# A graph and attention layer: the pass over node rows is taken into the blocks of the edge sort

## What is computed

```python
xn = layernorm(x)
h = xn @ W_layer.T + b_layer            # 6250 x 256, gathered once an edge
a1 = h @ w_a1.T + b_a1;  a2 = h @ w_a2.T + b_a2
v = leaky_relu(a1[src] + a2[dst])       # softmax over the edges of a src
gnn = segment_sum(att[:, None] * h[dst], src)
q, k = (elu(xn @ w + b) + 1 for the q and the k weights)
kv, k_sum = k.T @ v of each head, sum over nodes of k
x = x + gnn + (q @ kv / (q @ k_sum)) @ wo + bo
x = x + ffn(layernorm(x))
```

## Time and profile before

| | us |
|---|---|
| median of 3 runs | 2029.47 |
| the profiled execution | 2033.18 |
| its span, first to last instruction | 2031.4 |
| busy in it: PE / DVE / POOL / ACT | 1497.9 / 1424.6 / 1080.7 / 628.8 |
| mean granted PE clock, share of full | 0.855 |

### The profile page before, as it was taken

How to read it: one execution, slowest core, us unless ns; L and a number is a source line. 1 busy time by engine, 2 the same in 40 slices (tenths; PEclk the granted TensorE clock), 3 DMA queues, 4 the chain that set the end, 5 groups by cost and what they waited for, 6 DMA issues and landing times. The chain is left out here.

```text
span 2031.4 us, 28833 instructions
## 1 busy us (share of the span) xinstructions
PE 1497.9 (74%) x8525; PEld 1175.0 (58%) x8525; DVE 1424.6 (70%) x4324; ACT 628.8 (31%) x1738; POOL 1080.7 (53%) x1147
## 2 busy tenths in 40 slices
PE   5555555348878758887888877887877878887699
PEld 3333333247767636666666666666666666665477
DVE  7888888865555538777777777877777778776244
ACT  0000000024344315444444444444444445442000
POOL 0245555501111057777777777777777777771000
PEclk8666666579999959888889899989998999989689
DMA  9500000001111134444444444444444444451622
GB/s 118 93 3 4 3 4 3 3 21 47 48 47 47 44 97 118 116 126 118 118 121 123 117 117 121 119 117 117 128 117 117 116 123 119 120 146 37 237 83 73
DMA packets 118495, 180.08 MB, mean 89 GB/s; under 512 B 41704, under 2 KB 90395, under 8 KB 118364
## 3 DMA queue, kind: packets, MB, share of 16 engines
q0 software_dynamic: 44384, 113.26, 21.7%
q1 hardware_dynamic: 62891, 45.40, 10.4%
q10 hardware_dynamic: 11088, 19.87, 2.6%
HBM read 143.16 MB, written 35.29 MB: 88 GB/s over the span
## 5 line engine op out<-in xcount | busy, mean ns | idle before, releaser
L978 POOL DMA_INDIRECT big<-node_table,rest x850 | 853.2, 1004 | 243.9 <-issue 231.2
L1049 PE MATMUL psum<-big 128*125 128x257 f32 x1700 | 460.4, 431 | 107.1 <-DVE big L1511 107.1
L1049 PEld LDWEIGHTS psum<-big 128*125 128x125 f32 x1700 | 360.0, 217 | 179.2 <-DVE big L1511 114.0
L1183 ACT ACTIVATE rest<-big,rest 128x125 f32<-128x125 bf16 x850 | 268.3, 490 | 184.4 <-DVE rest L1459 184.4
L321 POOL DMA_INDIRECT edge_groups<-rest x112 | 170.7, 1524 | 188.8 <-DVE rest L691 159.0
L1511 DVE TENSOR_SCALAR big<-big,rest 128x125 f32<-128x125 bf16 x850 | 173.6, 294 | 0.0
L342 POOL TENSOR_TENSOR X<-X,big 125x256 f32<-125x256 f32 x50 | 31.8, 638 | 260.5 <-DVE rest L778 260.5
L400 PE MATMUL psum<-rest 128*128 128x128 f16 x784 | 84.7, 304 | 111.7 <-DVE rest L676 111.7
L400 PEld LDWEIGHTS psum<-rest 128*128 128x128 f16 x784 | 78.5, 143 | 123.6 <-issue 82.0
L1077 PE MATMUL psum<-rest,big 125*128 125x126 f32 x416 | 72.0, 326 | 91.9 <-DVE big L1430 91.7
L1466 DVE TENSOR_REDUCE rest<-rest 128x125 f32<-128x2125 f32 x50 | 118.3, 2367 | 30.4 <-ACT rest L1183 30.4
(11 more groups left out here) (377 smaller groups left out, 2793.3 us busy)
## 6 DMA issues: line engine op xcount, KB each, us to landing
big<-node_table,rest POOLq DMA_INDIRECT x850
slice_weights<-rest ACTq DMA_DIRECT2D x52, 252.0 KB, 3.0
big<-slice_weights ACTq DMA_DIRECT2D x25, 252.0 KB, 7.0
big<-slice_weights SPq DMA_DIRECT2D x25, 252.0 KB, 6.7
node_table<-rest SPq DMA_DIRECT2D x50, 126.0 KB
query_features<-rest SPq DMA_DIRECT2D x50, 125.0 KB, 2.0
rest<-query_features SPq DMA_DIRECT2D x50, 125.0 KB, 2.5
out_dram<-rest SPq DMA_DIRECT2D x50, 125.0 KB
```

The source lines that it names most:

```text
L978: pool.indirect_dma_start(Gt[:, u, q * TW:(q + 1) * TW], None, table, bass.IndirectOffsetOnAxis(ap=item[:, u, 2 * q:2 * q + 1], axis=0)).t ...
L1049: mm = pe.matmul(bank[bAgg][0:R, 0:D + 1], P[:, u, q, :], Gt[:, u, q * TW:q * TW + D + 1], start=q == 0, stop=q == Q - 1)
L1183: act.activation(V[:, :, q], O[:, u, q, 0:R], ACT.Copy, scale=score[:, u, q:q + 1]).then_inc(s_v, 1)
```

## The change

- **The pass over node rows** is cut into units of one tile, spread over sort blocks 2 to 13: five tiles in blocks 2 and 8, four in each other one (`UNITS`). PE runs the units between the sort's own steps: the first after `ranks(4n+3)`, the middle ones after `ranks(4n+5)`, the last between the two halves of `put`. ACT normalises, copies the transpose, makes both parts of k's feature and copies h, a2 and a1 out of PSUM; POOL adds the two parts and keeps their sum (`k_features`) between its scatters. DVE has no part in a unit. Biases come from a bf16 matmul with three rows (`ones3` by `row3`) ahead of each product, and `va` is part of `WT`, now 259 columns wide.
- `ranks(g)` waits on `chosen` instead of `selected`.
- Flags of items come from 50 columns and one matmul (`items`), in sort block 0; the statistics lie behind the first two sort blocks, unrolled; the bias rows and normalisers are made in block 1.
- **Query features** are no longer stored: the turned xn is (`xn_store`), with the same DMA size, and in the gather loop PE makes q of tile i+2 (`queries`), DVE its lower part (`query_below`), ACT the exponent (`query_exp`) and DVE the feature (`query_feature`) of tile i+1. `bo` is added in `mix` by a matmul, so POOL's L342 is gone.

```diff
+                    def k_features(t):
...
+                        pool.wait_ge(ke_done, t + 1)
...
+                        pool.tensor_tensor(ks[:, u, :], re[:, u, 0, :], re[:, u, 1, :], ALU.add).then_inc(ks_done, 1)
+                        pool.wait_ge(ks_done, t + 1)
...
+                        pool.tensor_tensor(ks_sum, ks_sum, ks[:, u, :], ALU.add).then_inc(acc_done, 1)
...
+                    for m in range(1, NB + 1):
+                        units = UNITS[m] if m < NB else []
+                        c = 0
+                        for i, t in enumerate(units):
+                            k_features(t)
+                            for _ in range(2 if i < 3 else 0):
+                                scatter(m - 1, c)
+                                c += 1
+                        for c in range(c, GC):
+                            scatter(m - 1, c)
...
-                    pool.wait_ge(weights_in, 16 * 15)
-                    for t in range(T):
-                        pool.wait_ge(xn_done, t + 1)
-                        pool.tensor_tensor(X[:, t, :], X[:, t, :], bo, ALU.add).then_inc(bo_added, 1)
...
-                            pe.wait_ge(selected, g - 1)
+                            pe.wait_ge(chosen, g - 1)
...
+                    def turn(t):
...
+                            pe.wait_ge(kr_done, 2 * t)
...
+                    def key_products(t):
...
+                        pe.wait_ge(ks_done, t + 1)
+                        for c in range(DC):
+                            mm = pe.matmul(bank[6][:, c * D:(c + 1) * D], ks[:, t % 2, c * 128:(c + 1) * 128], xn[:, t % 4, :],
+                                           start=t == 0 and c == 0, stop=t == T - 1, skip_group_check=True)
+                    def unit(t):
...
+                        u = t % 2
+                        pe.wait_ge(xnT_done, t + 1)
+                        pe.matmul(bank[0][0:R, D:2 * D], ones3, row3[:, BK_AT:BK_AT + D], start=True, stop=False)
+                        for c in range(DC):
+                            mm = pe.matmul(bank[0][0:R, D:2 * D], xnT[:, u, c, :], wk[:, c, :], start=False, stop=c == DC - 1)
+                        mm.then_inc(k_psum, 1)
+                        if t:
+                            pe.wait_ge(a12_done, t)
+                        pe.matmul(bank[7][0:R, 0:D + 3], ones3, row3[:, 0:D + 3], start=True, stop=False)
+                        for c in range(DC):
+                            mm = pe.matmul(bank[7][0:R, 0:D + 3], xnT[:, u, c, :], WT[:, c, :], start=False, stop=c == DC - 1)
+                        mm.then_inc(h_psum, 1)
+                        if t >= 2:
+                            key_products(t - 2)
+                        if t < T - 1:
+                            turn(t + 1)
 
...
                     for n in range(NB):
-                        block_starts(n)
-                        for g in range(GPB * n + 2, min(GPB * n + GPB + 2, NB * GPB)):
-                            ranks(g)
-                        put(n)
-                    pe.wait_ge(edges_ready, 2 * NB)
-                    pe.wait_ge(weights_in, 16 * 15)
-
+                        ranks(GPB * n + 2)
+                        ranks(GPB * n + 3)
+                        for t in UNITS[n][0:1]:
+                            unit(t)
+                        if n + 1 < NB:
+                            ranks(GPB * n + 4)
+                            ranks(GPB * n + 5)
+                        if n == 0:
+                            items()
+                        if n == 1:
+                            table_weights()
+                        for t in UNITS[n][1:-1]:
+                            unit(t)
+                        if n + 1 < NB:
+                            pe.wait_ge(moved_made, 3 * (2 * n + 1))
+                            block_starts(n + 1)
+                        put(n, 0)
+                        for t in UNITS[n][-1:]:
+                            unit(t)
+                        put(n, 1)
+                    for t in range(T - 2, T):
+                        key_products(t)
...
+                    def normalise(t):
...
+                        if t >= 4:
+                            act.wait_ge(kx_psum, t - 3)
+                        act.activation(xn[:, t % 4, :], X[:, t, :], ACT.Identity, bias=shift[:, t:t + 1],
...
+                    def key_parts(t):
...
+                        act.wait_ge(k_psum, t + 1)
+                        if t >= 2:
+                            act.wait_ge(ks_done, t - 1)
+                        act.activation(below, bank[0][0:R, D:2 * D], ACT.Relu, scale=-1.0).then_inc(kr_done, 1)
+                        act.activation(above, bank[0][0:R, D:2 * D], ACT.Relu).then_inc(kr_done, 1)
+                        act.wait_ge(kr_done, 2 * t + 2)
+                        act.activation(below, below, ACT.Exp, scale=-1.0).then_inc(ke_done, 1)
...
+                    def table_rows(t):
...
+                        act.wait_ge(h_psum, t + 1)
...
+                        act.copy(ht[:, t % 2, :], bank[7][0:R, 0:D + 3]).then_inc(h_done, 1)
+                        act.copy(A12[:, t, :], bank[7][0:R, D + 1:D + 3]).then_inc(a12_done, 1)
...
+                    for t in range(T):
+                        turned(t)
+                        if t < T - 1:
+                            normalise(t + 1)
+                        key_parts(t)
+                        table_rows(t)
...
+                    step(dve.tensor_scalar(item_cmp, begun, group_id[:, 0:1], None, ALU.is_le))
+                    dve.tensor_reduce(item_col, item_cmp, AX, ALU.add).then_inc(item_made, 1)
...
+                        if k == 0:
+                            dve.wait_ge(x_in, 32)
+                            statistics(0, T // 2)
+                            item_flags()
+                        if k == 1:
+                            statistics(T // 2, T)
+                            normalisers()
...
+                    def queries(m, v, k):
+
+                        pe.wait_ge(xn_here[v], 16 * (k + 1))
+                        for i in range(DC):
+                            for c in range(DC):
+                                mm = pe.matmul(bank[bAgg][:, Q_AT + i * R:Q_AT + (i + 1) * R], wq[:, c, i * 128:(i + 1) * 128],
+                                               xn_in[:, v, c, :], start=c == 0, stop=c == DC - 1)
+                        mm.then_inc(q_psum, 1)
...
+                        pe.wait_ge(q_made, DC * m)
...
+                        pe.matmul(bank[bMix][0:R, MIXED_AT:MIXED_AT + D], ones3[:, 0:R], row3[:, BO_AT:BO_AT + D], start=True,
+                                  stop=False)
...
-                        norms(i + 1, v, k)
+                        norms(i + 1)
...
+                        if ahead:
+                            queries(i + 2, w, kv)
...
+                    def query_below(m):
...
+                        dve.wait_ge(q_psum, U + m)
+                        dve.wait_ge(q_made, DC * (m - 1))
+                        for c in range(DC):
+                            dve.tensor_scalar(q_exp[:, c, :], bank[bAgg][:, Q_AT + c * R:Q_AT + (c + 1) * R], bq[:, c:c + 1],
+                                              0.0, ALU.add, ALU.min).then_inc(q_low, 1)
...
+                    def query_feature(m):
...
+                        dve.wait_ge(q_expd, m)
+                        dve.wait_ge(qn_done, U + m - 1)
+                        for c in range(DC):
+                            dve.scalar_tensor_tensor(q_in[:, c, :], bank[bAgg][:, Q_AT + c * R:Q_AT + (c + 1) * R],
+                                                     bq1[:, c:c + 1], q_exp[:, c, :], ALU.add, ALU.max).then_inc(q_made, 1)
...
+                        query_below(i + 1)
...
+                        query_feature(i + 1)
```

573 lines of the change are left out of this document (269 added, 304 removed).

## The result

| | kernel before | changed kernel |
|---|---|---|
| median of 4 runs | 2029.89 us (2029.36 to 2031.49) | 1748.09 us (1744.85 to 1749.8) |
| ratio, 95% interval | | 0.8609 (0.8594 to 0.8624) |
| profiled execution, its span | 2031.4 us | 1749.8 us, 1748.1 us |

The forecast was 1740 us, 8 us less. The stretches of the changed kernel's profile, cut where the earlier trace rows cuts the one before: sort block 0, block 1, blocks 2 to 13 up to the last `unpack`, the head, the way to the first gather, the gather loop from first to last gather, and the rest. Columns: the stretch, its us, busy us and count of each engine, the granted clock of PE, the DMA share, GB/s.

The account below looks back on a forecast made before the run. DVE was taken to bound the sort blocks and POOL the gather loop; 2031.4 - 315 + 29 - 5 + 1.5 = 1742 us of span, 1740 us forecast, with 8 in 10 from 1708 to 1802.

Parts of the forecast that it names:

- What goes: Between sort and gather loop: of 333.0 us, 18 stay for `unpack`, eight scatters and POOL's masks; 315 us gone.
- Blocks 0 and 1: Sort blocks 0 and 1: statistics, flags, normalisers and bias rows add 29 us on DVE (26 to 40).
- The sort's block: Blocks 2 to 13: DVE's 23.3 us a block decides over PE's 22.0; sort total, with blocks 0 and 1's gain, -5 us.
- rival D: Sort blocks: additions cost DVE nothing, PE bounds at 22.0 us; 1715 to 1728 us, chance 0.12.
- rival E: Sort blocks: units wait for one another, 30 us a block, 1823 us; chance 0.05 for "E and between".
- rival A: Sort blocks lengthen to 26 to 29 us because PE's order ties three engines; 1772 to 1808 us, chance 0.22.
- rival C: PE lacks full clock: sort blocks take 43 us, 1976 us, or 2051 with a slow gather loop; chance 0.02.
- The gather loop: POOL sets 22.35 us an item; DVE's added 1.2 us fits its 2.6 us slack, so 0 for 50 items.
- Rival B: Gather loop no longer POOL's: 0.5 to 1.5 us an item more, 1765 to 1815 us, chance 0.13.
- from the head to the first gather: Stretch between head and gather loop: no term of its own, taken over unchanged at 6.9 us.
- the end: Last items of the gather loop, where no gather hides them: + 1.5 us.

Follow-up runs that it names:

- best_a: Changed kernel with no drain, masks early, first item's load earlier, key sums on PE, all statistics in block 1: ratio 0.9022, beside the changed kernel's 0.9090 on that chip.
- experiment 3: Changed kernel with PE's ranks waiting on `selected` again instead of `chosen`: 1774.33 us, ratio 0.8726.
- no_adds: Changed kernel with both POOL additions for a tile replaced by one-column memsets (output differs): 1724.94 us, ratio 0.8477.
- no_drain: Changed kernel with the first block of the program ending without POOL's DRAIN: 1747.28 us, ratio 0.8585.

## Why the prediction came out right, step by step

**What goes: right, its terms less so.** 315 us with 18 left; 18.8 were left. The order was as said: eight scatters nothing hides, then POOL's masks. But POOL came to these scatters only 3.5 us behind the last `unpack` (it had two of the block before to issue), which the sum didn't have, and from their end to the head's end were 5.5 us, not 7. DVE waited for the masks:

```profile
414.49 0.49 DVE L887 TENSOR_TENSOR big<-psum,big 128x128 f32<-128x128 f32 x2 [10.95 <-POOL rest L376]
```

**Blocks 0 and 1: the terms near, one missing.** Statistics 2 x 8.26 = 16.5 (17 forecast), flags 1.8 (2.5), normalisers 3.3 (4.7), bias rows 5.5 (4.5). Not in the sum at all was the load of X, which stands behind other loads:

```profile
68.17 8.26 DVE L801 BATCH_NORM_STATS2 rest<-X 125x6 f32<-125x256 f32 x25 [2.63 <-DMA X<-in_x_dram]
```

2.6 us here, and 1.4 to 9.4 in the nine other executions with this order; with all statistics in block 1 it is gone (blocks 0 and 1 in `best_a`: 67.8 and 67.7 us). It was covered in this profile because the ranks' earlier release gave 3.1 and 3.8 us in these two blocks (by subtraction; `choose`'s waits for PE in them fell from 8.2 to 1.0 us), where I had 1.5 each.

**The sort's block: the mechanism right, DVE's sum right, PE's too high.** DVE 20.35 + 0.3 without additions is 20.65; measured 20.7. Additions 2.6, measured 2.2: four a block, as taken, at 0.53 instead of 0.64. That it is four of eight was a guess, and a lucky one: with the ranks released later it was three (experiment 3). Together 23.3, measured 22.9. PE 22.0, measured between its 20.0 of busy time and 20.7; it was too high by 1.3 to 2.0 and cost nothing, because DVE decides. The stretches of five tiles took 26.6 and 24.5, against 26.7 twice. The rival D (1715 to 1728), additions free and PE the bound, falls with `no_adds`, rival E (30 us a block) with the blocks of 22.9, rival A with `choose`'s waits of 9.4 us in 12 blocks and 0.8 us for a scatter's landing, rival C with the clock of 0.98.

**The gather loop: right on the first chips,** within what five executions differ by. Rival B did not come there.

**The step that failed: from the head to the first gather.** The sum took the stretch over unchanged, 6.9 us. The row that shows it moving was in the trace before, but no view of busy time or waits lists it: POOL's DRAIN, 9.2 us, hidden by a head that ran 22 us longer than POOL. The change put POOL last, and the drain lay bare: 6.0 us. I asked of each step what the scatters and masks cost, but not what the barrier behind them waits for. The other 0.5 of the 6.5 us is there without the drain too (7.4 us to the first gather in `no_drain`) and was not traced.

**A term too small: the end.** 1.5 us was for the last items; five executions have 194.8 to 199.2, a mean of 196.5, 3.9 more than 192.6. In the first profile it lies between the last gather and the end of the last product of `sum_edges` (28.1 us before, 32.1 after; 30.4 to 32.1 in the five); from there to the end it is 164.6 and 164.7 (164.4 to 168.0 in the five). More than one item runs there without POOL's cover, and each carries DVE's 1.2 us and PE's 1.2, which would make it up; no run on the first chips tested that.

## What to carry to other kernels

When a change takes work out from between an engine's last instruction and a barrier, look at what that engine's queue still does there: instructions that count as no work (here a drain of 9.4 us) have a price as soon as the engine is the last to arrive. An addition that is moved to POOL isn't free for DVE, if it falls beside operations of DVE that read their operands from on-chip memory: here 0.53 us for each that met a product of `spread`, half of them all. Where it falls is set by what it waits for. And look at which event releases a wait: one word, `chosen` for `selected`, was worth 24 us here, half of what `choose`'s waits in the kernel before had promised.
